# Softmax normalisation moved into the values product's copy, and the output projection accumulated over a batch

## The reference, cut to what matters

```
q, k, v = (split_heads(x @ W) for W in (Wq, Wk, Wv))      # 16 heads of 64
q, k = apply_rope(q), apply_rope(k)
sim = where(causal, einsum('bid,bjd->bij', q, k) * 0.125, -inf)
attn = softmax(sim, axis=-1)
out = einsum('bij,bjd->bid', attn, v)                     # heads joined again
x = layernorm(x + out @ Wo + bo)
x = layernorm(x + ffn(x))                                 # 8 experts, top 2, gelu
```

## Time and profile before

| what | value |
|---|---|
| median of 3 runs | 805.34 us (800.24 to 806.1) |
| the profiled execution, its own time | 798.51 us |
| its span, first to last instruction | 796.7 us |
| TensorE busy | 755.9 us, 95% |
| VectorE busy | 667.4 us, 84% |
| ScalarE busy | 592.2 us, 74% |
| GpSimd busy | 572.0 us, 72% |
| mean granted TensorE clock | 0.997 |

### The profile page before, as it was taken

How to read it: one execution, slowest core, us unless ns; L and a number is a source line. 1 busy time by engine, 2 the same in 40 slices (tenths; PEclk the granted TensorE clock), 3 DMA queues, 4 the chain that set the end, 5 groups by cost and what they waited for, 6 DMA issues and landing times.

```text
span 796.7 us, 20539 instructions
## 1 busy us (share of the span) xinstructions
PE 755.9 (95%) x5763; PEld 535.0 (67%) x5763; DVE 667.4 (84%) x2514; ACT 592.2 (74%) x1678; POOL 572.0 (72%) x701
## 2 busy tenths in 40 slices
PE   8899999999999999999999989999998899999995
PEld 4455666666666566666666656666656579999995
DVE  6688888999899879998999899989987974235997
ACT  3688878878878777877887768777877756565677
POOL 3686767558765877677768886976786266989983
PEclk9999999999999999999999999999999999999998
DMA  4576666456755566556555655565557667434525
GB/s 152 188 224 200 214 203 201 165 191 197 227 180 174 174 200 195 188 180 210 175 186 191 194 173 186 186 199 173 177 179 225 222 193 207 109 85 125 163 90 163
DMA packets 110719, 144.66 MB, mean 182 GB/s; under 512 B 13392, under 2 KB 86352, under 8 KB 110608
## 3 DMA queue, kind: packets, MB, share of 16 engines
q1 hardware_dynamic: 106240, 134.49, 53.8%
q0 software_dynamic: 4224, 8.72, 3.3%
q10 hardware_dynamic: 144, 0.13, 0.1%
HBM read 61.42 MB, written 45.17 MB: 134 GB/s over the span
## 4 chain that ended last, share of the span: by engine, by line
PE 67%; POOL 13%; DVE 8%; issue 7%; DMA 3%; ACT 1%; SPq 0%; DVEq 0%; POOLq 0%; ACTq 0%
PE AO L1109 15%; PE S_all L1068 14%; PE TB L1089 9%; PE AO L1129 5%; PE S_all L1256 4%; POOL yrows L956 4%; PE TB L1269 2%; POOL shared L973 2%; PE AO L1269 2%; DVE Sm L1609 2%; DMA qk<-shared 2%; DVE x_acc L1630 1%; PE TB L1000 1%; POOL shared L722 1%; PE TB L998 1%
## 5 line engine op out<-in xcount | busy, mean ns | idle before, releaser
L1376 ACT ACTIVATE Pr_all<-Sm,nmax 128x512 f32<-128x512 f32 (+3 forms) x512 | 281.8, 563 | 23.7 <-DVE nmax L1609 22.9
L1609 DVE CUSTOM_DVE_ANT_0 Sm<-S_all,causal 128x512 f32<-128x512 f32 (+3 forms) x512 | 223.0, 482 | 46.0 <-PE S_all L1068 45.9
L1068 PE MATMUL S_all<-qk 64*128 64x512 f32 (+3 forms) x1024 | 169.8, 446 | 10.9 <-DVE nmax L1609 8.6
L717 POOL TENSOR_TENSOR qk<-shared,qk 128x512 f32<-128x512 f32 x64 | 81.9, 1280 | 129.6 <-DMA qk<-shared 119.9
L1109 PE MATMUL AO<-PT,shared 128*64 128x128 f32 x1008 | 149.6, 438 | 13.1 <-issue 12.7
L1386 ACT ACTIVATE PT<-TB 128x768 f32<-128x768 f32 x189 | 107.8, 605 | 61.2 <-PE TB L1089 61.2
L1630 DVE SCALAR_TENSOR_TENSOR x_acc<-AO,rinv,x_acc 128x128 f32<-128x128 f32 x504 | 141.7, 344 | 3.5 <-POOL x_acc L769 1.3
L1068 PEld LDWEIGHTS S_all<-qk 64*128 64x128 f32 x1024 | 79.7, 187 | 82.6 <-issue 56.9
L1089 PE MATMUL TB<-ident,Pr_all 128*128 128x128 f32 x764 | 109.2, 279 | 3.6 <-ACT PT L1386 3.1
L1089 PEld LDWEIGHTS TB<-ident,Pr_all 128*128 128x128 f32 x764 | 82.0, 141 | 44.4 <-issue 40.6
L1109 PEld LDWEIGHTS AO<-PT,shared 128*64 128x64 f32 x1008 | 66.5, 136 | 61.1 <-issue 30.9
(11 more groups left out here) (335 smaller groups left out, 1459.0 us busy)
## 6 DMA issues: line engine op xcount, KB each, us to landing
turns<-turned_pr SPq DMA_DIRECT2D x63, 512.0 KB
PT<-turns SPq DMA_DIRECT2D x252, 128.0 KB
qk<-shared SPq DMA_DIRECT2D x124, 256.0 KB
wo<-in_wo SPq DMA_DIRECT2D x64, 64.0 KB, 3.1
PT<-yrows SPq DMA_DIRECT2D x7, 512.0 KB, 4.3
w_tile<-in_wup SPq DMA_DIRECT2D x10, 256.0 KB, 3.5
xt<-xrows SPq DMA_DIRECT2D x32, 65.0 KB, 2.7
x_acc<-in_x SPq DMA_DIRECT2D x8, 256.0 KB, 3.4
```

The lines of the kernel that those rows point to most:

```text
L717: nc.gpsimd.tensor_tensor(qT[p][:, :], q_cos, qT[p][:, :], ALU.add).then_inc(q_ready, 1)
L1068: nc.tensor.matmul(SB[2 * (group % 2) + h][:, at:at + (qb + 1) * P], qT[p][half, qb * P:qb * P + P], kT[p][half, 0:(qb + 1) * P], start=Tr ...
L1376: nc.scalar.activation(Pr[j][:, 0:n], Sm[j], ACT.Exp, bias=nmax[:, j:j + 1], scale=-1.0, accum_out=rsum[p][:, h * QB + qb:h * QB + qb + 1] ...
L1609: nc.vector.tensor_tensor_reduce(out=Sm[j], in0=SB[2 * (group % 2) + h][:, at:at + n], in1=causal[:, T - n:T], scale=-0.125, scalar=HUGE, ...
```

## The change

Between the values product and the output projection the softmax is now normalised. After `invert(u)` VectorE transposes the reciprocals (8 columns of a tile of 32) within blocks of 32. SyncE's queue stores them in DRAM (`norms`), waits until they are there, and loads them so that partition d of a head's 64 holds the reciprocals of all 512 tokens (`spread_norms`). VectorE multiplies the values product by them on its way out of PSUM (`norm_o`), in place of ScalarE's copy. The output projection needs no factor of its own any more: it is one matmul over both heads' 128 rows for each block of tokens, and adds up in one PSUM bank over the 8 units of a batch; `add_y` adds the sum to `x_acc` once a batch. Unit 63 keeps the old way (`project_last`, `scale_y`).

The squares' layout in DRAM is changed, so that one transfer loads them in place of four. The weights of the output projection stay in SBUF from unit 8 on. Scores of all groups are issued in one run, group 2 into the bank of the transposes, and the output projection follows them. In SyncE's queue the unit's store, swaps and load come ahead of the weights, x and rows, and `spread_norms(u - 1)` ahead of the store.

The diff, cut to its core:

```diff
-LOADED = LANES * 16
+LOADED = 16
...
+        def spread_of(u):
+
+            if u < PAIRS:
+                e = E - 2 + u % 2
+                return wdown[:, e * IB:e * IB + IB, :].rearrange("p a c -> p (a c)")
+            return hT[u % 2][:, :]
...
+        rinv, rinv_turned = (st2[:, i, :, :].rearrange("p n s -> p (n s)")[:, 0:SQ] for i in range(2))
...
+        v_later = SB[2]
...
-        def y_bank(u):
-            return (SB[2], SB[3]) if u == UNITS - 1 else (AB, OB)
+        y_bank, last_y = OB, (SB[2], SB[3])
...
-            two = TB if u < UNITS - 1 or group == 0 else S_all[:, 2 * group - 2:2 * group, :]
+            two = S_all[:, 0:2, :] if group == 1 else S_all[:, 2:4, :] if group == 2 and u == UNITS - 1 else TB
...
+        def score_bank(group, h):
+            return TB[:, h, :] if group == 2 else SB[2 * group + h]
+
+        def wo_of(u):
+
+            if u < PAIRS or u % PAIRS >= 6:
+                return wo[u % 2][:, :]
+            return w_tile[u % PAIRS // 4][:, u % 4 * P:u % 4 * P + P]
...
-                wait(sp, y_done, u - 1)
-                sp.dma_start(wo[p][:, :], wo_h[bass.ds((u % PAIRS) * P, P), :]).then_inc(wo_in[p], 16)
                 if first:
                     load_x(0)
+                elif u <= PAIRS:
+                    load_wo(u - 1)
+                if not first:
+                    spread_norms(u - 1, 1 - p)
+                if not last:
+                    store_turned(u, p)
+                if first:
+                    load_turned(u, p)
+                if u + 2 < UNITS:
+                    swap(u + 2, p)
+                if not first and not last:
+                    load_turned(u, p)
+                if u == PAIRS:
+                    keep_wo()
...
-                if not last:
-                    store_turned(u, p)
-                if first:
-                    load_turned(u, p)
-                if u + 2 < UNITS:
-                    swap(u + 2, p)
-                if not first and not last:
-                    load_turned(u, p)
...
-            def store_turned(u, p):
-
-                sp.wait_ge(turned, 2 * u + 2)
-                wait(sp, turns_in, LOADED * (u - 1))
-                sp.dma_start(turns[p * P:p * P + P, :], turned_pr[:, :, :, :].rearrange("p b c s -> p (b c s)")).then_inc(stored, 16)
-
-            def load_turned(u, p):
-
-                sp.wait_ge(stored, 16 * (u + 1))
-                wait(sp, pv_done, u - 1)
-                squares = turns[p * P:p * P + P, :].rearrange("(a r) (b n) -> b r a n", r=SQ, b=LANES)
-                for b in range(LANES):
-                    sp.dma_start(PT[p][SQ * b:SQ * b + SQ, LANES * (QB - 1):, :, :].rearrange("k a c s -> k a (c s)"),
-                                 squares[b]).then_inc(turns_in, 16)
+            def load_wo(u):
+
+                wait(sp, y_done, u - 1)
+                sp.dma_start(wo[u % 2][:, :], wo_h[bass.ds((u % PAIRS) * P, P), :]).then_inc(wo_in[u % 2], 16)
+
+            def keep_wo():
+
+                rows = wo_h.rearrange("(n p) c -> p n c", p=P)
+                sp.wait_ge(q_proj, PAIRS)
+                sp.wait_ge(k_proj, PAIRS)
+                sp.wait_ge(w_split, PAIRS // 2)
+                for i, (first, end) in enumerate(((0, 4), (4, 6))):
+                    to = w_tile[i][:, 0:(end - first) * P].rearrange("p (n c) -> p n c", c=C)
+                    sp.dma_start(to, rows[:, first:end, :]).then_inc(wo_in[0], 16)
...
+            def spread_norms(u, p):
+
+                sp.wait_ge(inverted, 2 * u + 2)
+                wait(sp, norms_in, 16 * (u - 1))
+                sp.dma_start(norms[p * SQ:p * SQ + SQ, :].rearrange("c (a r) -> a c r", r=SQ), rinv_turned).then_inc(norms_stored, 16)
+                sp.wait_ge(norms_stored, 16 * (u + 1))
+                wait(sp, norms_in, 16 * u)
+                wait(sp, o_ready, u - 1)
+                if u == PAIRS:
+                    sp.wait_ge(q_proj, PAIRS)
+                    sp.wait_ge(k_proj, PAIRS)
+                    sp.wait_ge(w_split, PAIRS // 2)
+                heads = norms[p * SQ:p * SQ + BLK, :].rearrange("(h q) t -> h (q t)", h=2)
+                sp.dma_start(spread_of(u), heads.unsqueeze(1).to_broadcast([2, D, T])).then_inc(norms_in, 16)
+
+            def store_turned(u, p):
+
+                sp.wait_ge(turned, 2 * u + 2)
+                wait(sp, turns_in, LOADED * (u - 1))
+                sp.dma_start(turns[p * P:p * P + P, :].rearrange("(r a) n -> a r n", a=LANES),
+                             turned_pr[:, :, :, :].rearrange("p b c s -> p (b c s)")).then_inc(stored, 16)
+
+            def load_turned(u, p):
+
+                sp.wait_ge(stored, 16 * (u + 1))
+                wait(sp, turns_in, LOADED * u)
+                wait(sp, pv_done, u - 1)
+                squares = turns[p * P:p * P + P, :].rearrange("(r a) (b n) -> b (r a) n", a=LANES, b=LANES)
+                sp.dma_start(PT[p][:, LANES * (QB - 1):, :, :].rearrange("k a c s -> k (a c s)"), squares).then_inc(turns_in, 16)
...
-                if u == 2:
-                    pe.wait_ge(v_ready, 2)
-                elif u > 2:
-                    pe.wait_ge(pt_ready, 2 * (u - 3) + 1)
+                if u >= 2:
+                    pe.wait_ge(maxed, BLK * (u - 1))
...
-                    pe.wait_ge(y_read, 2 * (u - 4) + 1)
+                    pe.wait_ge(o_ready, u - 3)
...
-                    pe.wait_ge(pt_ready, 2 * u + 1)
+                    pe.wait_ge(maxed, BLK * (u + 2))
                 else:
-                    wait(pe, pt_ready, 2 * u)
-                    pe.wait_ge(q_read, min(u + 3, UNITS))
-                    if u == 0:
-                        pe.wait_ge(k_read, 2)
+                    pe.wait_ge(maxed, BLK * (u + 1) + DONE_BY[0])
...
             def project_out(u, p):
-                pe.wait_ge(wo_in[p], 16 * (u // 2 + 1))
+                if u < PAIRS:
+                    pe.wait_ge(wo_in[p], 16 * (u // 2 + 1))
+                elif u == PAIRS:
+                    pe.wait_ge(wo_in[0], 16 * (PAIRS // 2 + 2))
 
                 pe.wait_ge(o_ready, u + 1)
-                if u == UNITS - 1:
-                    pe.wait_ge(pt_ready, 2 * UNITS)
-                    pe.wait_ge(maxed, BLK * UNITS)
-                    pe.wait_ge(routed, ROUTE * (B - 2) + RANKS_READ)
-                else:
-                    pe.wait_ge(v_ready, min(QB + u + 1, VBLOCKS))
-                    if u >= VBLOCKS - QB:
-                        pe.wait_ge(y_read, 2 * u)
+                first, last_pair = u % PAIRS == 0, u % PAIRS == (PAIRS - 1 if u < UNITS - 2 else PAIRS - 2)
+                if first:
+                    if u == 0:
+                        pe.wait_ge(v_ready, QB)
+                    else:
+                        pe.wait_ge(y_read, u // PAIRS)
+                for i in range(QB):
+                    last = nc.tensor.matmul(y_bank[:, i * P:i * P + P], OT[p][:, i * P:i * P + P], wo_of(u),
+                                            start=(first and i == 0), stop=last_pair, skip_group_check=True)
+                last.then_inc(y_done, 1)
...
-                wait(pe, maxed, BLK * u)
+                wait(pe, maxed, BLK * (u - 1) + DONE_BY[1])
+                wait(pe, pt_ready, 2 * (u - 2) + 1)
...
                 score(u, p, 1)
-                pe.wait_ge(maxed, BLK * u + DONE_BY[0])
+                if first:
+                    project_k(u + 2, *second)
+                    pe.wait_ge(k_read, 2)
+                    pe.wait_ge(v_ready, 2)
+                else:
+                    pe.wait_ge(maxed, BLK * u)
+                    wait(pe, pt_ready, 2 * (u - 1))
+                    pe.wait_ge(q_read, min(u + 2, UNITS))
                 score(u, p, 2)
+                if u >= 2:
+                    project_out(u - 2, p)
...
-                if u >= 2:
-                    copy_o(u - 2, p)
...
-                wait(dve, y_read, 2 * u)
-                nc.vector.reciprocal(rinv[:, :], rsum[p][:, :]).then_inc(inverted, 1)
+                nc.vector.reciprocal(rinv[:, 0:BLK], rsum[p][:, :]).then_inc(inverted, 1)
+                if u < UNITS - 1:
+                    dve.wait_ge(inverted, 2 * u + 1)
+                    wait(dve, norms_stored, 16 * u)
+                    nc.vector.transpose(rinv_turned, rinv).then_inc(inverted, 1)
+
+            def norm_o(u, p):
+
+                dve.wait_ge(pv_done, u + 1)
+                dve.wait_ge(norms_in, 16 * (u + 1))
+                wait(dve, y_done, u - 1)
+                nc.vector.tensor_tensor(OT[p][:, :], o_bank(u), spread_of(u), ALU.mult).then_inc(o_ready, 1)
+
+            def add_y(b):
+
+                dve.wait_ge(y_done, min(PAIRS * (b + 1), UNITS - 1))
+                dve.wait_ge(x_set, b + 1)
+                rows = x_acc[:, b * QB:b * QB + QB, :].rearrange("p a c -> p (a c)")
+                nc.vector.tensor_tensor(rows, y_bank, rows, ALU.add).then_inc(y_read, 1)
...
+                if u >= 2:
+                    norm_o(u - 2, p)
```

(27 more changed lines are left out.)

74 lines of the change are left out of this document (37 added, 37 removed).

## The result

The changed kernel takes 1745.35 us (median of 4 runs, 1735.97 to 1751.55), the kernel before 803.05 us in the same comparison (800.24 to 806.1). The ratio is 2.172, with a 95% interval of 2.157 to 2.188. The forecast was 1560 us with a range of 1380 to 1790; the measured time is 12% above its centre and inside the range.

The account below looks back on a forecast made before the run. TensorE's 9.18 of 9.81 us a unit bound the kernel before; confined transfers would bind after. First load at 35.2, 62 x 21.9 = 1358, then 160.5 + 5: span 1558.5, plus 1.8 gives 1560 us, range 1380 to 1790.

Parts of the forecast that it names:

- The root: Squares' transfers and spreading load: confined to no more engines than outermost steps, 4 and 2; chance 0.85, near 1560 us.
- The chain: DMA engines 0 and 1: load, small store, spread and store can't overlap, 21.9 us a unit (18.8 to 26.3).
- the load's data: Squares' load, a quarter (128 KB) on each of four engines: taken 6.7 us a unit, 5.1 to 8.3.
- the spread's data: Spreading load of the norms, half (128 KB) on each of two engines: taken 6.0 us, 5.1 to 8.3.
- the part of the store left behind the spread: Squares' store, queued behind the spread: a quarter, 128 KB at 25.6 GB/s, 5.1 us a unit.
- The ends: Kernel's start and finish: first load lands at 35.2 us; 160.5 + 5 us follow the load of unit 62.
- What would show it: Profile signs: DMA share 4/16 and 2/16, store-to-load gap over 6 us, values product waiting 12, TensorE under half busy.
- The masks: VectorE's queue: norm_o and reciprocal ahead of them fit in 1.0 us, costing nothing while products arrive in time.
- The rival on all engines: All 16 engines work on every transfer shape: about 780 us, faster than before; chance 0.10.
- given back: SyncE's queue and masks: waiting 0.3 us a unit takes back the gain, 799 us, no change; chance 0.01.
- Squares alone confined: Only the squares' store and load on 4 engines: 16.9 us a unit, 1250 us; partly confined cases 0.04.
- Broadcast alone: Only the spreading load confined, on 2 engines: 13.7 us a unit, 1045 us; partly confined cases 0.04.

Follow-up runs that it names:

- old_squares: Changed kernel with the squares' DRAM order, store and four loads of the kernel before, spread still on two engines: 1147.9 us.
- before_one_load: Kernel before with only the squares' new DRAM order, stored and loaded by one transfer each of outermost dimension 4, no spread: 1226.6 us.
- wide_spread: Changed kernel with the spreading load cut into two transfers, each with 64 partitions outermost: 1572.7 us.
- one_load_before_load: wide_both with the same unit's small store between swaps and load, squares written by four stores and read by one load of 128 rows: 798.9 us, ratio 0.992.
- norms_behind_swap: wide_both with the wait for the small store and the spread moved behind the swaps in SyncE's queue: 1070.4 us, ratio 1.329.
- wide_both: Changed kernel with squares stored and loaded as in the kernel before and the spread in two transfers of 64 partitions: 862.2 us, ratio 1.074.

## Why the prediction was right, and by how much its terms were off

**The root held.** The spans of time show four engines for the squares and two for the spread, and undoing the two shapes takes away 883 of 942 us. This was the judgement on which 0.85 of the chance lay.

**The chain held, each term was somewhat too small.** I gave a unit 21.9 us; it takes 24.6, and 24.8 up to unit 62. From the issues in the queue and the first and last piece of each transfer in the trace, as medians over the units:
- the load's data: 6.7 forecast, 7.1 measured;
- small store and the gap to the spread's first data: 2.4 forecast, 2.6 measured;
- the spread's data: 6.0 forecast, 6.9 measured. Its 2 KB pieces take 84 ns at first and some 130 ns while the swaps run;
- from there to the next load's first data, that is the part of the store left behind the spread, its landing and the start of the load: 5.1 + 1.7 = 6.8 forecast, 7.9 measured.

The pace of an engine was not the fault. I had taken 19.6 GB/s for each in the load and 25.6 in the store; the load's four move 88, or 22 each, over 824.00 to 829.50, the spread's two 24.5 each in old_squares, the store's four 26 each in before_one_load. What the terms lacked is that a confined transfer does not keep this pace throughout: it starts slowly (the load moves 63 GB/s from 824 to 825 us and 96 from 826 to 829), and the spread slows down beside the swaps. The store suffers most: started at once it takes 9.4 us, and 5.1 was priced. That the forecast came within 12% is partly luck: in the changed kernel the store stands behind the spread during its slow time, and only 1.1 us of the error is left in the unit. Where the spread is quick, in wide_spread, the same price is wrong by 3.0 us a unit: 9.8 us pass from the spread's last data to the next load's first, against 6.8.

**The ends.** The values product of unit 0 starts at 40.76 where I had its load land at 35.2, mostly for the same reason: the first store took 9.4 us and not 5.1. From unit 62's values product to the end it is 171.4 us (165.5 forecast). 5.6 + 62 x 2.9 + 5.9 = 191 us is the whole distance from 1558.5 to the span of 1749.8.

**What would show it.** The share fell to 4/16 at 88 GB/s (forecast: some 100) and 2/16. The issue of a load follows its store by 13.9 us (over 6). TensorE is busy 51 to 56% of the attention's stretches of 100 us and not under half; its matmuls take longer where the lower clock is granted (4.18 us for a values product in place of 2.37). The projection takes 1.24 us at 840.28 and not 0.89; on a kernel without the waits, one_load_before_load, the next step starts 0.99 us after it. The values product waits 8 us a unit and not 12, because another 3 us of waiting stand before the projection.

**The masks: wrong.** I had the first mask 1.1 us after the first score and norm_o free of cost. In the changed kernel it comes at 840.51, 5.7 us after the scores at 834.83, because norm_o stands ahead of it and waits for the spread. It cost nothing there, since the turns had to wait for the squares' store anyway:

```profile
840.51 0.68 DVE L1678 CUSTOM_DVE_ANT_0 Sm<-S_all,causal 128x512 f32<-128x512 f32 x1
...
845.57 1.30 DVE L1657 STREAM_TRANSPOSE turned_pr<-Pr_all 128x512 f32<-128x512 f32 x2 [1.70 <-DMA turns<-turned_pr]
```

In norms_behind_swap this same order of VectorE's queue closed a loop of 14 us.

**The rival on all engines: wrong by 82 us.** It was to be 780; wide_both takes 862. Of the rivals the one "given back" named the right place, SyncE's queue standing for the small store's landing, but priced it at 0.3 us a unit and called it decided by whether the spread lands in time. The runs show about 1 us a unit: the queue's issues and landings add up to a loop longer than TensorE's. I had priced the added transfers by their data (0.7 us of DMA time) and not the queue by its length. *Squares alone confined* (forecast 1250) is wide_spread and came out at 1573, 21.8 us a unit in place of 16.9, for the store's slow start above; the 1227 of before_one_load is another kernel, without the spread. *Broadcast alone* (forecast 1045) is old_squares and came out at 1148.

## What to carry to other kernels

Before one transfer takes the place of several, write down the outermost dimension of both of its sides. If it is 2 or 4, the transfer has 2 or 4 engines, and it holds up what waits for it and what stands behind it on them. Here three saved issues a unit, 1.5 us, cost 424 us in all. One load with 128 rows outermost cost nothing; but its rows had to be written by four stores, so it saved no issue. Before a step with a wait is put into an in-order queue, follow the loop through every queue until it comes back to the step, and add up latencies along it; the two moves that I made without doing so cost 208 and 82 us.

## What the runs showed that I had not expected

A store of 512 KB on four engines that starts at once takes 9.4 us with next to nothing beside it, 55 GB/s in the mean, and it is the same with the rows next to each other or apart in DRAM. Yet the same four engines move 104 GB/s when the store has stood behind a load first (before_one_load, 62 to 66 us). The slow pieces go with the time since the store's issue; why is not settled. The pieces of the confined spread also slowed down, from 84 to some 130 ns, while the swaps ran; that cause is not settled either.
